# Cross attention's end and a quantised feed-forward: tokens and gates rounded in place, outputs in five parts, clearing and weights' rounding moved

## The reference, cut to what matters

```python
x = x + _L1_xattn_ref(_layernorm(x, axis=-1), ctx_768, Wq, Wk, Wv, Wo, bo)
x = x + _L1_ffn_ref(_layernorm(x, axis=-1), clip_x, clip_down, w_gate, w_up, w_down)

def _act_fake_quant(x, clip_factor):
    scale = jax.nn.sigmoid(clip_factor) * jnp.max(jnp.abs(x)) / QMAX
    return jnp.clip(round(x / scale), -QMAX - 1.0, QMAX) * scale

def _weight_fake_quant(w):
    scale = jnp.max(jnp.abs(w), axis=1, keepdims=True) / QMAX
    return jnp.clip(round(w / scale), -QMAX - 1.0, QMAX) * scale

xq = _act_fake_quant(x, clip_x[0])
gate = einsum('bsh,ih->bsi', xq, _weight_fake_quant(w_gate))
up = einsum('bsh,ih->bsi', xq, _weight_fake_quant(w_up))
h = _act_fake_quant(silu(gate) * up, clip_down[0])
return einsum('bsi,hi->bsh', h, _weight_fake_quant(w_down))
```

## Time and profile before

| what | value |
|---|---|
| time, median of 3 runs | 713.22 us (712.99 to 713.23) |
| the profiled execution | 711.25 us |
| its span, first to last instruction | 709.4 us |
| TensorE busy (matmuls) | 618.0 us, 87% of the span |
| VectorE busy | 572.3 us, 81% |
| ScalarE busy | 488.6 us, 69% |
| GpSimd busy | 383.0 us, 54% |
| mean granted TensorE clock | 0.96 of full speed |

### The profile page before, as it was taken

One profiled execution on the slowest core, in us unless ns is written; L12 is line 12 of the kernel. 1 busy time (PEld: TensorE's weight loads), 2 busy tenths in 40 slices (PEclk: granted clock), 3 DMA queues, 4 the chain that ended last, 5 costly groups with the idle time before them and its releaser, 6 DMA issues.

```text
span 709.4 us, 15973 instructions
## 1 busy us (share of the span) xinstructions
PE 618.0 (87%) x5514; PEld 432.4 (61%) x5547; DVE 572.3 (81%) x1457; ACT 488.6 (69%) x1423; POOL 383.0 (54%) x419
## 2 busy tenths in 40 slices
PE   3699997889999989998999998998899999996533
PEld 2465654556666666655666666766677777765212
DVE  4667778999999886879999997646777777785586
ACT  2677776778888873478888887335777777773333
POOL 4968767999999911859999992111122121202300
PEclk9999999999999999999999999999999999996575
DMA  7510000111111120011111110000000000000002
GB/s 229 148 32 1 1 5 9 23 25 23 24 24 24 23 62 16 8 46 35 24 24 24 25 24 17 1 2 0 2 2 1 1 2 1 2 1 1 0 0 60
DMA packets 20219, 17.28 MB, mean 24 GB/s; under 512 B 7234, under 2 KB 15884, under 8 KB 20044
## 3 DMA queue, kind: packets, MB, share of 16 engines
q1 hardware_dynamic: 19308, 16.25, 9.0%
q10 hardware_dynamic: 832, 0.00, 0.1%
HBM read 8.91 MB, written 1.05 MB: 14 GB/s over the span
## 4 chain that ended last, share of the span: by engine, by line
PE 65%; DVE 18%; ACT 9%; issue 7%; DMA 0%; POOL 0%; POOLq 0%; DVEq 0%; SPq 0%; ACTq 0%
PE PS L818 9%; PE PS L1008 5%; PE PS L1033 4%; PE PS L870 4%; PE PS L989 4%; PE PS L845 3%; PE PS L1018 3%; PE PS L892 3%; PE PS L910 3%; PE PS L911 3%; DVE rsin L1617 3%; PE PS L827 3%; PE PS L823 2%; ACT pc L1240 2%; PE PS L772 2%
## 5 line engine op out<-in xcount | busy, mean ns | idle before, releaser
L1240 ACT ACTIVATE pc<-PS,nb,rsq 128x128 f32<-128x128 f32 x256 | 113.9, 463 | 0.9 <-DVE nb L1631 0.3
L818 PE MATMUL PS<-wqkv,hB 128*128 128x512 f32 x192 | 103.2, 621 | 4.4 <-DVE rsin L1617 2.4
L1313 ACT ACTIVATE pc<-PS,nb 128x256 f32<-128x256 f32 x128 | 58.9, 472 | 43.7 <-DVE nb L1815 43.7
L507 POOL TENSOR_TENSOR rsk<-btmp,neghalf 128x8 f32<-128x8 f32 x32 | 61.0, 1908 | 5.9 <-POOL btmp L502 5.9
L1815 DVE TENSOR_REDUCE nb<-PS 128x2 f32<-128x512 f32 x64 | 41.1, 685 | 25.8 <-PE PS L1008 25.8
L827 PEld LDWEIGHTS PS<-ident,rot 128*128 128x128 f32 x256 | 31.1, 141 | 43.7 <-issue 17.2
L507 POOL TENSOR_TENSOR rsq<-btmp,neghalf 128x8 f32<-128x8 f32 x32 | 53.6, 1674 | 5.9 <-POOL btmp L502 5.9
L1640 DVE TENSOR_TENSOR pc<-pc,rden 128x512 f32<-128x512 f32 x64 | 53.4, 835 | 2.2
L1240 ACT ACTIVATION_READ_ACCUMULATOR pc<-PS,nb,rsq 128x1 f32 x256 | 53.8, 210 | 0.0
L1613 DVE TENSOR_TENSOR rot<-PS,xeff 128x512 f32<-128x512 f32 x64 | 44.0, 688 | 6.8 <-ACT sq L1228 6.3
L1826 DVE TENSOR_SCALAR pc<-pc,rden 128x256 f32<-128x256 f32 x128 | 47.5, 413 | 2.3
(11 more groups left out here) (237 smaller groups left out, 1713.5 us busy)
## 6 DMA issues: line engine op xcount, KB each, us to landing
V<-V SPq DMA_DIRECT2D x48, 128.0 KB, 2.2
wqkv<-in_L_ffn_wqkv SPq DMA_DIRECT2D x2, 768.0 KB, 5.4
out<-x SPq DMA_DIRECT2D x4, 256.0 KB, 2.3
x<-in_x SPq DMA_DIRECT2D x1, 768.0 KB, 6.8
ctxT<-in_ctxT SPq DMA_DIRECT2D x1, 768.0 KB, 7.2
w<-in_L_ffn_w SPq DMA_DIRECT2D x2, 341.0 KB
ctxs<-in_ctx SPq DMA_DIRECT2D x1, 576.0 KB, 8.3
gel<-in_bands SPq DMA_DIRECT2D x1, 512.0 KB, 8.4
```

Source lines behind the costliest of these rows:

```text
L507: return tt(dst, tmp, neghalf[:, 0, 0:tmp.shape[1]], ALU.pow)
L818: i = mm(ps, hB[:, b % 2, j * P:(j + 1) * P], wqkv[:, w * INNER:(w + 1) * INNER], start=True, stop=True)
L1240: i = af(pc[:, g % 2, par, c * P:(c + 1) * P], c_bank(g, par)[:, c * P:(c + 1) * P], ACT.Exp, bias=nb[:, g % 2, at], scale=rsq[:, g % 8, 2 ...
L1313: i = af(pc[:, u % 2, par, n * S:(n + 1) * S], c_bank(u, par)[:, n * S:(n + 1) * S], ACT.Exp, bias=nb[:, u % 2, par * 2 + n:par * 2 + n + ...
```

## The change

VectorE's weights' steps 0 to 4 stand in the fourth unit of batches 2 to 6. GpSimd clears after unit 31's probabilities are made. The output product of batch 7 is made for each tile by itself (`c_last`), the first before the values of unit 31, together with the turning of the gate and up weights; its tokens are made by tile (`c_last_tokens`). The buffer `hq` is laid out by group. All tokens are multiplied, clipped and rounded in place in y by VectorE; `zqb` has four buffers, and turned tokens two banks. ScalarE rounds gates group 1 (multiply, add `ROUND`) and VectorE only clips it. The output is made in five parts, batches 0-1, 2-3, 4-5, 6 and 7, each with its own bank, and five stores.

```diff
+OUT_PARTS = [(0, 2), (2, 4), (4, 6), (6, 7), (7, 8)]
-        hq = big[:].rearrange("p (c t) -> p c t", c=3)
+        hq = big[:].rearrange("p (g c t) -> p g c t", g=4, c=3)
...
-            with sp.Fori(0, 4) as g:
-                sp.wait_ge(sem("y_out"), g + 1)
-                sp.dma_start(out[bass.ds(g * 2, 2)].rearrange("b (j p) d -> p (b j) d", p=P),
-                             x[:, bass.ds(g * 4, 4), :]).then_inc(sem("stored"), 16)
+            for n, (blo, bhi) in enumerate(OUT_PARTS):
+                sp.wait_ge(sem("y_out"), n + 1)
+                sp.dma_start(out[blo:bhi].rearrange("b (j p) d -> p (b j) d", p=P),
+                             x[:, blo * 2:bhi * 2, :]).then_inc(sem("stored"), 16)
...
             for par in range(2):
-                pool.wait_ge(s_full[par], C_UNITS[-1] + 1)
-            nc.gpsimd.memset(hq[:, 2, :], 0.0).then_inc(sem("D_zero"), 1)
-            pool.wait_ge(sem("C_xst"), B)
-            rsqrt(rt[:, 0:2], mvt[:, 0:2, 1], rtmp[:, 0:2], 1e-5, ALU.add, "C_xtmp", B).then_inc(sem("C_xr"), 1)
-
-            pool.wait_ge(sem("D_scale"), 1)
-            for g in range(1, 4):
-                yb = y[:, g * 4:g * 4 + 4, :]
-                ts(yb, yb, sc[:, 7:8], QMAX, ALU.mult, ALU.min).then_inc(sem("D_q0"), 1)
+                pool.wait_ge(p_full[par], C_UNITS[-1] + 1)
+            nc.gpsimd.memset(hq[:, :, 2, :], 0.0).then_inc(sem("D_zero"), 1)
+            for j in range(2):
+                pool.wait_ge(sem("C_last_st"), j + 1)
+                rsqrt(rt[:, 2 + j:3 + j], mvt[:, 2 + j:3 + j, 1], rtmp[:, 2 + j:3 + j], 1e-5, ALU.add, "C_xtmp", B + j) \
+                    .then_inc(sem("C_last_r"), 1)
...
+            def c_last(j):
+
+                ps, k, turn = c_piece("W", B - 1)
+                pe.wait_ge(bank_free[k], 2 * turn)
+                if j:
+                    pe.wait_ge(sem("C_last_x"), 1)
+                pe.wait_ge(sem("chain_o_free"), C_UNITS[(B - 1) * C_STEPS + 2 * j + 1] + 1)
+                for c in range(4):
+                    i = mm(ps[:, j * D:(j + 1) * D], oT[:, (B - 1) % 2, j, c, :], woC[:, c, :], start=(c == 0), stop=(c == 3))
+                i.then_inc(sem("C_last_W"), 1)
...
+                if n == len(C_UNITS) - 1:
+                    c_last(0)
+                    pe.wait_ge(sem("D_wq"), 1)
+                    for par in range(2):
+                        pe.wait_ge(pT_full[par], u)
+                    for k in range(2):
+                        for c, (c0, m) in enumerate(QCH):
+                            turned = tr(psb(k)[:, c0:c0 + m], wqb[0:m, k, c, :], identb[0:m, 0:m])
+                    turned.then_inc(sem("D_wT"), 1)
                 c_values(u)
...
-            c_make("W", B - 1)
-
-
-            for par in range(2):
-                pe.wait_ge(pT_full[par], C_UNITS[-1] + 1)
-            pe.wait_ge(sem("chain_o_free"), C_UNITS[-1] + 1)
-            c_wait_copied(B - 1, "k01", "k23", "W")
-            pe.wait_ge(sem("D_wq"), 1)
-            for k in range(2):
-                for c, (c0, m) in enumerate(QCH):
-                    tr(psb(k)[:, c0:c0 + m], wqb[0:m, k, c, :], identb[0:m, 0:m])
             for c, (c0, m) in enumerate(QCH):
                 tr(psb(2)[0:m, c * P:(c + 1) * P], wdb[:, c0:c0 + m], identb[:])
             mm(PS[:, 3, 0:D], ones[:], diag[:], start=True, stop=True).then_inc(sem("D_wT"), 1)
+            c_last(1)
+            c_wait_copied(B - 1, "k01", "k23")
+            pe.wait_ge(sem("C_last_x"), 2)
...
-                    if c == 0 and g < 3:
-                        d_turn(g + 1)
+                if g < 2:
+                    d_turn(g + 2)
...
             d_turn(0)
+            d_turn(1)
...
-            d_tokens(0)
-            d_copy(0)
-            d_tokens(1)
+            d_tokens(0)
+            d_tokens(1)
+            d_copy(0)
+            d_tokens(2)
             act.wait_ge(sem("D_scale"), 1)
...
-                    if c == 0 and g < 3:
+                    if (g, c) in ((0, 2), (1, 1), (2, 1)):
                         d_copy(g + 1)
-                    if c == 1 and g < 2:
-                        d_tokens(g + 2)
+                    if (g, c) == (1, 0):
+                        d_tokens(3)
+
+            act.wait_ge(sem("D_s"), 9)
+            af(hq[:, 1], hq[:, 1], ACT.Identity, scale=sc[:, 15:16], bias=posr[:, 0:1]).then_inc(sem("D_h1a"), 1)
+            for n, (blo, bhi) in enumerate(OUT_PARTS):
+                g = blo // 2
                 act.wait_ge(sem("D_hr"), g + 1)
+                at = slice(blo % 2 * S, blo % 2 * S + (bhi - blo) * S)
+                af(hqbs[g][:, :, at], hq[:, g, :, at], ACT.Identity, bias=negr[:, 0:1]).then_inc(sem("D_hq"), 1)
...
+            def c_last(j):
+
+                ps, k, turn = c_piece("W", B - 1)
+                t = T - 2 + j
+                dve.wait_ge(sem("C_last_W"), j + 1)
+                dve.wait_ge(sem("C_bias"), B)
+                tt(x[:, t, :], ps[:, j * D:(j + 1) * D], x[:, t, :], ALU.add).then_inc(sem("C_last_x"), 1)
+                dve.wait_ge(sem("C_last_x"), j + 1)
+                nc.vector.bn_stats(bstf[:, 2 + j, :], x[:, t, :]).then_inc(sem("C_last_bn"), 1)
+                dve.wait_ge(sem("C_last_bn"), j + 1)
+                nc.vector.bn_aggr(mvt[:, 2 + j, :], bstf[:, 2 + j, :]).then_inc(sem("C_last_st"), 1)
...
-                if b == B - 2 and i >= 1:
-                    quantise_weights(i - 1)
-                if b == B - 1 and i < 2:
-                    quantise_weights(i + 3)
-                if b == B - 1 and i >= 1:
+                if i == C_STEPS - 1 and B - 6 <= b < B - 1:
+                    quantise_weights(b - (B - 6))
+                if b == B - 1 and i in (1, 2):
                     magnitudes((i - 1) * 4, i * 4)
-            c_residual(B - 1)
+                if b == B - 1 and i == 2:
+                    magnitudes(8, T - 2)
+                    c_last(0)
+            c_last_tokens(0)
+            for k in range(2):
+                dve.wait_ge(sem("D_wT"), 1)
+                nc.vector.tensor_copy(wguT[:, k, :], psb(k)[:, 0:IQ]).then_inc(sem("D_wc"), 1)
+            c_last(1)
...
+                yg = y[:, g * 4:g * 4 + 4, :].rearrange("p j d -> p (j d)")
+                ts(yg, yg, sc[:, 7:8], QMAX, ALU.mult, ALU.min).then_inc(sem("D_q0"), 1)
                 dve.wait_ge(sem("D_q0"), g + 1)
+                ts(yg, yg, -QMAX - 1.0, ROUND, ALU.max, ALU.add).then_inc(sem("D_q1"), 1)
...
             d_quant(0)
+            d_quant(1)
+            d_quant(2)
             ts(gus[:, 0:6], wsc[:, 0:6], sc[:, 6:7], None, ALU.mult).then_inc(sem("D_scale"), 1)
...
+            def d_round(g):
+
+                r = hq[:, g]
+                if g == 1:
+                    dve.wait_ge(sem("D_h1a"), 1)
+                    ts(r, r, ROUND - QMAX - 1.0, ROUND + QMAX, ALU.max, ALU.min).then_inc(sem("D_hr"), 1)
+                else:
+                    ts(r, r, sc[:, 15:16], QMAX, ALU.mult, ALU.min).then_inc(sem("D_h1"), 1)
+                    dve.wait_ge(sem("D_h1"), max(g, 1))
+                    ts(r, r, -QMAX - 1.0, ROUND, ALU.max, ALU.add).then_inc(sem("D_hr"), 1)
...
+            d_round(0)
+            d_round(1)
+            d_round(2)
             ts(dsc[:], dsc[:], sc[:, 14:15], None, ALU.mult).then_inc(sem("D_s"), 1)
+            d_round(3)
+            for n in range(len(OUT_PARTS)):
+                d_out(n)
```

More of the change, by code:

```diff
@@ L51 @@
 FIRST = 1
-N_CONST = 6
+N_CONST = 7
 A_LOADS = 5
@@ L294, in program @@
         negr = sb("negr", [P, 1])
+        posr = sb("posr", [P, 1])
         mx = sb("mx", [P, 2, 8])
@@ L371, in f_bank, with d_bank @@
             return PS[:, (G % 4 * 3 + c) % 2 * 2 + k, :]
+        def d_bank(n):
+            return n
         block = ctx.enter_context(nc.Block())
@@ L492, in rest_of_constants @@
                 nc.gpsimd.memset(negr[:], -ROUND).then_inc(sem("const"), 1)
+                nc.gpsimd.memset(posr[:], ROUND).then_inc(sem("const"), 1)
                 nc.gpsimd.memset(wgu[:, :, 2, :], 1.0).then_inc(sem("const"), 1)
@@ L1118, in _, with d_down @@
             d_turn(0)
+            d_turn(1)
             for g in range(4):
                 d_up(g)
-            def d_down(g):
-                pe.wait_ge(sem("D_hq"), g + 1)
-                if g >= 1:
-                    pe.wait_ge(sem("D_yo"), g)
-                for j in range(4):
+            def d_down(n):
+                blo, bhi = OUT_PARTS[n]
+                g = blo // 2
+                pe.wait_ge(sem("D_hq"), n + 1)
+                for j in range(blo % 2 * 2, blo % 2 * 2 + (bhi - blo) * 2):
                     for c, (c0, m) in enumerate(QCH):
-                        i = mm(PS[:, 7, j * P:(j + 1) * P], hqb[0:m, g % 2, c, j * P:(j + 1) * P], wdT[0:m, c, :],
+                        i = mm(PS[:, d_bank(n), j * P:(j + 1) * P], hqbs[g][0:m, c, j * P:(j + 1) * P], wdT[0:m, c, :],
                                start=(c == 0), stop=(c == 2))
@@ L1132, in _ @@
             d_over_partitions(1)
```

(49 more changed lines are left out.)

55 lines of the change are left out of this document (21 added, 34 removed).

## The result

The changed kernel takes 695.28 us (median of 4, 694.49 to 697.2) against 713.11 us for the kernel before in the same session: ratio 0.976, 95% interval 0.9733 to 0.9788. The forecast was 698.5, with 696.6 to 704.2 as its range: the direction and most of the mechanisms are as forecast, but the gain is 17.8 us and not the 14.7 of the sum, and the time lies under the low end of the range. The profiled execution took 695.93 us with a span of 694.1, 15.3 us under that of before.

What follows compares the result with a forecast made beforehand. TensorE was busy through almost the whole span; the last 75 us were read engine by engine, with VectorE busy in gates and outputs. From 713.22, 2.6 + 4.3 + 1.85 + 1.1 + 4.8 + 0.1 = 14.7 us gave 698.5; range 696.6 to 704.2.

Steps and rivals of the forecast that it cites:

- wide rounding pair: Last rounding: VectorE's pair of instructions over 1536 columns in place, taken at 1.95 us, with bounds 1.8 and 2.4.
- a stall in batches 2 to 6: Rival: a moved weights' step stops TensorE in batches 2 to 6 and the clock falls; 716.5 us, chance 0.02.
- queued stores: Rival at the end: five stores queue up, or wide instructions take 2.4 us a pair; 700.0 us, chance 0.09.
- the softmax pair near 639: Sign in the last batch's softmax scaling: VectorE's pair of multiplies, 2.78 us before, would be back at 0.6 us.
- The first stage: Unit 31's scores to the maximum's product: gains of 2.6 us (moved work), 4.3 (split product) and 1.85 (normalisation's tail).
- The tokens and gates: Tokens rounded in place by VectorE, through the end of the gates: 1.1 us gained, gates ending at 685.3.
- The two waits in the gates: VectorE waiting for ScalarE in the first two groups of the last stage's gates: about 0.9 us together.
- The end: Last rounding and outputs, from 688.98 to the last sum: 12.7 us in place of 17.5, a gain of 4.8.
- The tail: Stores after the last sum: two more DMAs, the last half as large; 0.1 us gained.
- The first part: Weights' rounding and clearing moved: 1.12 and 2.17 us off VectorE's path, unit 30's values starting 2.6 us earlier.
- the split product: Output product in halves around the last values: 4.3 us gained at full clock, 0.6 us longer at half clock.
- half-clock case: Rival: clock falls before unit 30's values, split loses 0.6 us; 703.4 us, chance 0.30 together with a later fall (701.9).

Runs made afterwards that it cites:

- the second execution of the same code: The unchanged code of the changed kernel run once more, beside the kernel before: 695.19 us against 711.78, ratio 0.9757.
- the part alone: Kernel before with only the tokens' multiply and clip moved from GpSimd to VectorE, in place, with buffers, banks and order to match: 709.97 us against 710.89, ratio 0.9999.
- the kernel whose TensorE had worked without a wait since 646.26: Kernel before with only the last output product made by tile, first half and weights' turning before the last values: 706.66 us, ratio 0.9948.
- the kernel whose TensorE took up work at 647.49: Kernel before with only GpSimd's clearing moved behind unit 31's probabilities: 708.80 us, one execution.

## Why the prediction was right or wrong

Right, by its own steps: the stop before the values of unit 30 (1.75 us forecast, 1.68 measured) and their start, 4.87 us after the scores (4.86 forecast); the moved steps at no cost to the batches before (152.9 us in both); the clock held over the last units; the end of the output product, 10.97 us after the scores (10.9); the wide rounding pair (1.02 and 0.96 us with 0.03 between); GpSimd's clearing beside maxima, at 1.80 us. The rivals of a stall in batches 2 to 6 and of queued stores (256 KB still land in 2.3 us) did not come. Of the signs, the softmax pair near 639 came by half: the pairs of unit 30 took 1.02 and 0.61 us, the first beside GpSimd's work on the tokens.

Wrong is the size of the sum: 14.7 against 16.9 us in the changed stretch. In the second execution of the same code, where the clock did less well, the stretch gained 15.8, so part of the miss is the luck of the clock. The terms that were short:

- *The first stage*, 8.75 forecast and 9.43 measured. I had VectorE ready for the second half at 650.1, 0.6 us after the product. It took it 0.03 us after it, and the way from there to the maximum's product was 2.96 us, not 3.15.
- *The tokens and gates*, 1.1 against 1.8. The two waits in the gates were put at 0.9 us; the part alone shows 0.44, and the changed kernel 0.15, because its clock came back early; in its second execution it was 0.44 again.
- *The end*, 4.8 against 5.0 from 688.98 on.
- *The tail*, 0.1 against 0.7. I priced the last store by the landing of 256 KB, and gave half the size and the written-out stores next to nothing. They are worth 0.45 and 0.25.

Each error is 0.2 to 0.7 us, and all have one sign: where I followed a chain, I put its waits too long, and to the tail I gave next to nothing. A range whose low end lay 1.9 us under the forecast had no room for four such terms.

Two further steps failed, though the sum did not show them. The first part was costed as 2.17 us for the clearing and 1.12 us for the step ahead; in fact the step alone decides, because without it the pair no longer meets the clearing, and the clearing moved alone gives 1.74. And the split product "costs something by itself, and pays only with the clock": alone it gave 4.2 us in its stage at a clock that had fallen, with TensorE's wait filled and the clock back for the last values. My half-clock case for it, 703.4, kept the whole list at half clock and was too slow by this trace.

The rest of the 17.8 us, 0.9, is not in the changed stretch. The 16.6 us of the second session suggest that it is the clock in the unchanged stages, where the two profiled executions differ by 1.57 us at the landmark. The executions without a profile show no stages, so this stays argued.

## What to carry to other kernels

When TensorE's path has a stop near its end, price the clock together with the stop: here 2.6 us of waiting cost 7.6. Before shortening work, try useful products in the wait, or the same number of useless ones; 18 of these, with nothing else changed, gave 5 us. Parts that both keep the clock up do not add.

When a serial end is one engine's, follow that engine's list. Let all its inputs come from buffers of their own, and make the last store small.

## What the runs showed of the hardware

- Around the stop of 1.74 or 1.75 us before the scores of unit 31 the clock fell in one trace of fourteen, and in none of six at the stop of 1.68 or 1.69 us before the values of unit 30. It fell in or just behind every stop of 2.54 us (one trace) and of 2.92 us (five traces) that was not filled. It was back by 652 in the kernel whose TensorE had worked without a wait since 646.26, and before 651.96 in the kernel whose TensorE took up work at 647.49, just as it fell.
- A GpSimd multiply of 256 columns and a fill of 2048 columns behind it held VectorE's pair of 256-column multiplies from 0.61 to 2.78 us; the multiply alone made it 1.04. The fill did not hold maxima (1.29 us for two out of PSUM, as without it) or copies out of PSUM (0.42).
- GpSimd's sums of two SBUF tensors held VectorE's like sum from 0.69 to 1.73 us, and not its products out of PSUM (0.68).
- GpSimd's multiplies of 512 columns in the kernel before (665.50 to 671.45) did not hold VectorE's step on 512 columns at 667.99, which took 0.46 us.
- Unchanged stages differ between executions: the same code had a spell at half clock around 150 us in one profile and none in the other.
